# Latent attention scores: both tiles of a pair in row halves of TensorE for all three split terms

## What is computed

```python
kv_rope = kv_c * cos[None] + _rotate_half(kv_c) * sin[None]      # (32, 1500, 64)
scores  = einsum('bhsr,bhlr->bhsl', q_r, k_r)
attn    = softmax(scores, axis=-1)
ctx_c   = einsum('bhsl,bld->bhsd', attn, kv_rope)
```

## Time and profile before

| | us |
|---|---|
| median of 3 runs | 1911.01 |
| fastest and slowest run | 1903.14, 1913.05 |
| span of the profiled execution | 1905.6 |
| latent scores in it, first and last start (L2454) | 371.1, 1003.2 |
| busy in the span: PE, DVE, ACT, POOL | 1505.3, 1418.2, 1058.1, 638.9 |

### The profile page before, as it was taken

The page is one execution under the profiler, slowest core; times in us unless marked ns, Lnnn a source line. Parts: engine busy times, 40 slices in busy tenths (PEclk is TensorE's granted clock), DMA queues, the critical chain, the costliest instruction groups (busy, mean ns, idle before and its releaser), DMA issues. The chain is left out here.

```text
span 1905.6 us, 37670 instructions
## 1 busy us (share of the span) xinstructions
PE 1505.3 (79%) x12653; PEld 910.4 (48%) x12668; DVE 1418.2 (74%) x2445; ACT 1058.1 (56%) x1759; POOL 638.9 (34%) x653
## 2 busy tenths in 40 slices
PE   1777776999999999999996746880687859956792
PEld 0455553433333333333334635870466537735682
DVE  6888865789898999989986774435688736667574
ACT  1777754766666666666663333440567535536461
POOL 1222211244545545455420234551233210026242
PEclk9665656999999999999997767995799879968897
DMA  6920000112111121111200144434000010023334
GB/s 163 333 87 1 1 1 33 28 36 50 39 40 48 35 51 37 43 46 35 53 11 2 32 121 134 133 110 133 1 2 0 0 25 1 0 86 125 103 107 155
DMA packets 79003, 116.28 MB, mean 61 GB/s; under 512 B 12530, under 2 KB 59834, under 8 KB 78484
## 3 DMA queue, kind: packets, MB, share of 16 engines
q1 hardware_dynamic: 69011, 91.53, 17.0%
q0 software_dynamic: 7776, 21.28, 3.2%
q10 hardware_dynamic: 2112, 2.10, 0.3%
HBM read 59.74 MB, written 40.19 MB: 52 GB/s over the span
## 5 line engine op out<-in xcount | busy, mean ns | idle before, releaser
L2603 DVE TENSOR_TENSOR lat_dsum<-lat_dsum,lat_Pb 125x896 f32<-125x896 f32 x320 | 414.8, 1296 | 62.2 <-ACT lat_Pb L2537 56.1
L2537 ACT ACTIVATE lat_Pb<-banks 125x896 f32<-125x896 f32 x384 | 331.4, 915 | 175.7 <-PE banks L2460 175.0
L2415 PE MATMUL banks<-lat_Pb,lat_kv 125*64 125x448 f32 x1536 | 332.5, 554 | 0.0
L2454 PE MATMUL banks<-lat_QH,lat_kT 128*125 128x448 f16 x768 | 184.5, 363 | 2.7 <-DVE lat_QT L2561 1.9
L2370 POOL TENSOR_TENSOR lat_kk<-lat_rot,lat_kk 125x768 f16<-125x768 f32 x32 | 71.6, 2237 | 317.5 <-ACT lat_kk L2509 317.5
L2415 PEld LDWEIGHTS banks<-lat_Pb,lat_kv 125*64 125x64 f32 x1536 | 93.4, 136 | 154.2 <-issue 153.0
L2454 PEld LDWEIGHTS banks<-lat_QH,lat_kT 128*125 128x125 f16 x768 | 89.7, 137 | 114.8 <-ACT lat_Pb L2537 89.1
L2917 POOL DMA_INDIRECT sent_outputs<-moe_yb,moe_yidx x98 | 99.0, 1010 | 135.4 <-ACT moe_yb L3174 108.4
L3055 PE MATMUL banks<-moe_w2d,moe_gT 88*128 (+3 forms) x780 | 103.9, 285 | 18.7 <-DVE moe_gT L3392 10.0
L2460 PE MATMUL banks<-lat_QL,lat_kT 64*125 64x448 f16 x768 | 114.2, 376 | 0.0
L3380 DVE COPY moe_xTb<-banks 128x1024 f16<-128x1024 f16 x49 | 33.7, 689 | 92.0 <-PE banks L3022 59.7
(11 more groups left out here) (440 smaller groups left out, 3291.2 us busy)
## 6 DMA issues: line engine op xcount, KB each, us to landing
moe_xb<-sent_rows SPq DMA_DIRECT2D x49, 257.0 KB
lat_raw<-in_ctx_dram SPq DMA_DIRECT2D x32, 375.0 KB
sent_rows<-zero SPq DMA_DIRECT2D x1, 7453.0 KB, 47.9
lat_QH<-lat_QT SPq DMA_DIRECT2D x64, 112.0 KB, 2.2
lat_QL<-lat_QT SPq DMA_DIRECT2D x64, 112.0 KB, 2.2
moe_arena<-sent_outputs SPq DMA_DIRECT2D x12, 512.0 KB, 6.5
sent_rows<-zero SPq DMA_DIRECT2D x1, 5140.0 KB, 64.4
sent_outputs<-zero SPq DMA_DIRECT2D x1, 4096.0 KB, 39.4
```

Source lines behind the costliest of these rows:

```text
L2415: ins = nc.tensor.matmul(ps[u * DC:(u + 1) * DC, 4 + par, 0:8 * T], kv[:, par, tt, :], Pb[:, tt % NPB, u, :], start=tt == 0, stop=tt == KT ...
L2454: nc.tensor.matmul(ps[0:KP, 2 * u + tt % 2, 0:8 * T], kT[:, par, tt, 0:KP], queries(QH, u), start=True, stop=False)
L2537: nc.scalar.activation(Pb[:, slot:slot + 2, u, :], ps[0:KP, 2 * u:2 * u + 2, 0:8 * T], ACT.Exp, scale=1.0 / QSCALE).then_inc(exp_done, 1)
L2603: ins = nc.vector.tensor_tensor(dsum[:, par], dsum[:, par], Pb[:, tt % NPB], ALU.add)
```

## The change

Key tiles are laid out the other way: `kk` and `kT` have for each pair one tile with the high parts of the even and the odd tile side by side (index 2a), and one with both low parts (index 2a+1). After the transposes rows 0 to 63 belong to the even tile and rows 64 to 127 to the odd one. All three terms are then half matmuls, six per u, in the order high x QH, low x QH, high x QL, each for the even and for the odd tile. The scores of u = 0 are finished, and announced on `s_done`, before those of u = 1 begin. The number of transposes, their shapes, the exponentials, the adds and all DMAs stay.

```diff
             def halves(par, low):
-                units = kk[:, par].rearrange("p (a q) u d -> p a (q u) d", q=2)
-                return units[:, :, 1:3, :] if low else units[:, :, 0:4:3, :]
+                return kk[:, par, low:KT:2, :]
 
             def paired(a):
-                return a.rearrange("p (a q) d -> p a q d", q=2)
+                return a.rearrange("p (a q) d -> p a (q d)", q=2)
...
-            kk = sb("kk", [KP, 2, KT, 2, DC], F16, c=main)
+            kk = sb("kk", [KP, 2, KT, 2 * DC], F16, c=main)
...
                                     pe.wait_ge(exp_done, b * KT + (2 * pair - 1 + u))
-                                for tt in both:
-                                    nc.tensor.matmul(ps[0:KP, 2 * u + tt % 2, 0:8 * T],
-                                                     kT[:, par, tt, 0:KP], queries(QH, u),
-                                                     start=True, stop=False)
-                            for u in range(2):
-                                for tt in both:
-                                    rows = slice(0, DC) if tt % 2 == 0 else slice(DC, P)
-                                    ins = nc.tensor.matmul(ps[0:KP, 2 * u + tt % 2, 0:8 * T],
-                                                           kT[rows, par, tt, 0:KP],
-                                                           queries(QL, u, rows),
-                                                           start=False, stop=True)
+                                for n, (low, Q) in enumerate(((0, QH), (0, QL), (1, QH))):
+                                    for q in range(2):
+                                        rows = slice(q * DC, (q + 1) * DC)
+                                        ins = nc.tensor.matmul(ps[0:KP, 2 * u + q, 0:8 * T],
+                                                               kT[rows, par, 2 * pair + low, 0:KP],
+                                                               queries(Q, u, rows),
+                                                               start=n == 0, stop=n == 2)
                                 ins.then_inc(s_done, 1)
```

More of the change, by code:

```diff
@@ L2403, in turn @@
                                 bank[:, n * KS:n * KS + KP],
-                                kk[:, par, tt].rearrange("p u d -> p (u d)"), id16[0:KP, 0:KP])
+                                kk[:, par, tt], id16[0:KP, 0:KP])
                         ins.then_inc(kT_done, 1)
@@ L2439, in body, with queries @@
                             return
-                        def queries(Q, u, rows=slice(0, P)):
+                        def queries(Q, u, rows):
                             return Q[rows, par, 8 * u:8 * u + 8, :].rearrange("p h t -> p (h t)")
                         for pair in range(KT // 2):
-                            both = (2 * pair, 2 * pair + 1)
                             for u in range(2):
```

## The result

The changed kernel takes 1948.57 us (median of 4 runs, 1947.98 to 1953.19), the kernel before 1910.20 beside it: a ratio of 1.0213 with an interval of 1.0191 to 1.0234, so 2.1% slower. The interval reaches from 1.9 to 2.3% and the runs of the two kernels don't overlap (the slowest one before took 1913.05), so the loss is clear of noise. The profiled execution has a span of 1946.1 us against 1905.6, which is +40.5 where I had worked out +51.

The account below looks back on a forecast made before the run. PE was taken to bound the loop, DVE 1.7 us behind. Five DVE-POOL collisions a batch give 27 x 2.00 = 54.0, less 1.8 and 0.9: +51 us on 1905.6, 1957, median 5.4 above: 1962, range 1893 to 1985.

Parts of the forecast that it names:

- Streams: PE's score matmuls: a pair streams 6 x 0.19 us before and after, nothing gained or lost, though 12 matmuls replace 8.
- Switches: PE's changes of matmul shape, 0.15 us each: four fewer a batch, so 0.60 us less, 19.81 to 19.21.
- Weight loads: PE's half matmuls: loads taken as hidden, no cost; at most 0.25 us a pair; rival that they don't hide 1940, chance 0.05.
- Earlier scores: u = 0 ready 0.78 us into the pair instead of 1.31; POOL asks for its subtract at 3.65 instead of 4.18.
- The subtract overtakes the first add: DVE and POOL: adds slide later, the subtract asked at 3.65 us gets ahead of the next add, and they alternate.
- the rival that keeps the gain: Subtract stays behind DVE's first add, which needs it before 3.65 us (expected 3.78): -19.5 us, 1891; chance 0.21.
- Prices of a collision: DVE add blocked by POOL: subtract 1.34 us, cosines 1.50, sines 0.68 each, sum 1.48; DVE's batch 20.33 with four, 21.81 with five.
- The sum: Whole loop, five collisions a batch: 54.0 - 1.8 - 0.9 = +51 us, so 1962; chance 0.40.
- a rival of its own, four collisions: Raw rows land just behind the first add's request, so one add passes free: +11 us, 1922; chance 0.19.
- above 1.5 us: Sign on DVE: the mean of the adds would exceed 1.5 us, where one alone takes 1.09.
- 2 us or more a batch: Sign on PE: idle time in front of L2426, ended by DVE's adds, of 2 us or more a batch.
- A slower clock on top: PE waits of 2 to 4 us a batch could lower the clock; only lengthens the five-collision case, to 1985.

Follow-up runs that it names:

- e2_light_after: Changed kernel with POOL's five loop instructions cut to one tile each: 1883.06 us, ratio 0.9905 to the kernel before.
- e11_wide_skip: Changed kernel with DVE's adds two tiles at a time and the second range check left out: 1887.29 us, ratio 0.9889 to the kernel before.
- e4_order: Changed kernel with the three terms in the outer loop and u inside, so scores of u = 0 come later: 1961.50 us, ratio 1.0304 to the kernel before.
- e5_subwait: Changed kernel with POOL's subtract also waiting for DVE's first add of its batch: 1901.72 us, ratio 0.9997 to the kernel before.
- e1_pad3: Changed kernel with the first score slot of pair 0 issued three more times per batch: 1901.22 us, ratio 0.9988 to the kernel before.
- e12_pad1: Changed kernel with the first score slot of pair 0 issued once more per batch: 1953.99 us, ratio 1.0246 to the kernel before.
- e3_drop: Kernel before, old layout, with its third split term (the half matmuls with QL) left out: 1957.34 us, ratio 1.0278 to the uncut kernel.

## Why the prediction was right, point by point

The forecast of slower, and its mechanism, came true: 1948.57 us for 1962 in a range of 1893 to 1985. What it had wrong is how many of the rounds have the fifth collision.

- **Streams, Switches.** Shown. Pair 0 takes 2.93 us as forecast, and PE's batch 19.23 for 19.21; e2_light_after and e11_wide_skip run all batches so.
- **Weight loads.** They hide: slots stand 0.19 apart. The Trainium skill (TensorE: Matmul & The Clock Gate, Part 3) has a load overlap matmuls in flight only where the row groups differ; each slot here fills both halves, so the loads of the next slot always meet a matmul in flight in their own rows. Yet these slots are no wider than those of the full matmuls, so by these traces the rule doesn't hold here.
- **Earlier scores.** POOL asks for the subtract at 3.66, forecast 3.65. But they aren't needed: e4_order, where it asks at 4.04, tips too.
- **The subtract overtakes the first add.** Shown in batch 2, by e5_subwait and by e1_pad3 against e12_pad1. My "it misses by 0.13" for the rival that keeps the gain was too kind: in batch 2 the first add comes at 4.13 after the batch's start, not 3.78, and misses by 0.47. Only at a PE batch of 19.41 does it come near (0.09).
- **Prices of a collision.** They hold: four collisions were worked out to 20.33 a batch, and rounds with four take 20.35; five to 21.81, and rounds with five take 21.97, as the batches of e3_drop and e4_order do (21.98).
- **The sum.** Here a term was mis-sized. "27 batches at 21.81 - 19.81 = +2.00" gives +54.0; batches 4 to 30 took 575.42 us, which is 40.6 more than 27 x 19.81. The price was right and the count wrong: 15 rounds of 27 have five collisions and 12 have four, and 15 x 2.16 + 12 x 0.54 = 38.9. What I had as a rival of its own, four collisions, decided "by some tenths around 6.9 us", is a state of the same run. Two signs came out low, in keeping with that: the mean add 1.48 for "above 1.5 us", and PE's wait in the loop 34.9 us in 28 batches, 1.25 each, for "2 us or more a batch".
- **What decides four or five.** It is decided anew in each batch, by the cosines against the first add. In the batches whose first add comes at about 6.7 us after their start, it goes free when the cosines start at 6.70 or later and is blocked when they start at 6.67 or earlier, without exception (e12_pad1 parts at 6.66 and 6.70, and has 22 rounds with five and 5 with four); what lets the cosines go there is the landing of the rows' DMA. A round with five runs 1.6 us over the one with four, so the first add of the batch behind it comes at 8.22, the cosines (7.58 or 7.84) are ahead of it, and there are five again. That next batch is the one of 23.4 to 23.5 us, or of 21.97 where the clock didn't fall. Why the rows land at times up to 0.7 us apart is open; I made no run for it.
- **A slower clock on top.** It came in the seven batches of 23.4 to 23.5 us alone. Behind the wait of 2.04 us in batch 10 the granted clock was 0.50 from 585 to 587 us, which is the lower level (1.2 GHz), and 0.72 over 5 us; the first slots of pair 2 start 0.36 us apart (584.30, 584.66), and that pair took 5.12 us where it takes 3.48. Pairs 1 and 2 of all seven took 11.4 us more than in batch 18. But little of that is in the 40.5. Where DVE sets the pace the round lasts 21.97 with the drop and without it (batches 10 and 18 above), and PE waits the less in the next batch: 0.87 us in batch 11. In e3_drop, too, pair 2 takes 3.01 us in some batches and up to 4.65 in others, and either kind of batch lasts 21.95 to 21.98. Only in batch 30 does the drop count, since PE doesn't wait in the last batch: it takes 23.41, and 21.78 in e4_order, without the drop. After a batch with the drop PE is so far back that the next first add comes at 6.7 again and four are possible; after a batch without it (18, 24, and all of e4_order) the next has five again.
- **The first three batches** took 58.27 us, -1.2 for the -1.8 expected, since the third already waits. The last batch took 15.42 to the first score of its last pair, against 16.14 before: -0.72 for five of its six changes of shape, of the -0.9 expected for all.

## What to carry to other kernels

Where two engines stand close behind the one that bounds, time saved on the bounding one is no gain until it is known where it leaves the others: here 0.6 us less on TensorE per batch moved a GpSimd instruction from just behind a VectorE instruction to just ahead of it, and the program lost 2%. Before such a change, list the pairs of instructions that exclude each other and which one stands first, and by how much; a lead of a few tenths is a cover that the change can take away. Prefer few long instructions on the engine that must not be blocked, with its idle time where the other's start falls (here the wide adds alone gave 0.2%, and 1.1% with 0.5 us less work on VectorE besides); a wait that only holds the intruder back moves the collision to the next place.

## What the runs showed of the hardware that I had not expected

- The exclusion between VectorE and GpSimd costs by order, not by amount. In e11_wide_skip POOL is busy 10.44 us of a batch and DVE's adds mostly keep their 2.01 to 2.03; in the changed kernel POOL is busy 10.74 and four adds grow by 0.7 to 1.5 us. The Trainium skill (SBUF — State Buffer, Who interferes with whom) says that issue order decides who blocks; the traces agree, with a subtract 0.16 behind an add (1.08) and 0.47 ahead of one (2.54).
- The loss comes in steps. VectorE's round takes 19.8 us with two collisions (TensorE's pace), 20.35 with four and 21.97 with five, and a few tenths of a microsecond, of TensorE's work or of a DMA's landing, decide which. A program with a third of the score terms left out ran 2.8% slower than the whole.
- The granted clock does not follow from one wait alone. A wait of about 2 us in pair 1 (pair 6.08 us long) was followed by half clock in batches 10 and 22 (pair 2 of 5.12) and by full clock in batches 18 and 24 (pair 2 of 3.48). And where VectorE sets the pace the lower clock cost nothing: 21.96 us a round with it, 21.97 without.
